# Attention and a mixture-of-experts layer on one core: query scores lead by ten pairs, two DMA loads change places on SyncE's queue, and the edges of the attention part are rewritten

## The reference

```
q, k, v = x @ w.T + b                    # 16 heads of 8 features
attn    = softmax(q . k / sqrt(8))       # 256 x 256 for each head and batch
y       = (attn @ v) @ w_o.T + b_o       # f of the first block

scores  = sigmoid(x @ gate_w.T)          # 32 experts in 8 groups
choice  = scores + e_bias                # best 4 groups, then best 6 experts
c       = scores of the 6 / their sum * 2.5
f of the second block = sum_e c[e] * relu(x @ up[e])^2 @ down[e]  +  the same with one shared expert of 256
```

## Time and profile before

| | us |
|---|---|
| median of three runs (range) | 515.81 (515.64 to 517.17) |
| the profiled execution | 516.76 |
| its span, first to last instruction | 514.9 |
| TensorE busy | 467.5 (91%) |
| VectorE busy | 399.8 (78%) |
| ScalarE busy | 362.2 (70%) |
| GpSimd busy | 227.9 (44%) |
| first key scores of batch 0, of batch 1, of batch 13 | 42.50, 57.68, 223.70 |

### The profile page before, as it was taken

One profiled execution on the slowest core, in us unless ns is written; L12 is line 12 of the kernel. 1 busy time (PEld: TensorE's weight loads), 2 busy tenths in 40 slices (PEclk: granted clock), 3 DMA queues, 4 the chain that ended last, 5 costly groups with the idle time before them and its releaser, 6 DMA issues.

```text
span 514.9 us, 10734 instructions
## 1 busy us (share of the span) xinstructions
PE 467.5 (91%) x3352; PEld 269.1 (52%) x3352; DVE 399.8 (78%) x1031; ACT 362.2 (70%) x723; POOL 227.9 (44%) x546
## 2 busy tenths in 40 slices
PE   2458999999999999998899899999999999999994
PEld 1213444444444444454346566666666676766662
DVE  3678788899999989989826769597886869597453
ACT  3415788877888978887847476868868687866551
POOL 6054233325434635230103644839385674716251
PEclk9555899999999999999979899999999999999998
DMA  6544244454344444330024244435354445536421
GB/s 201 163 136 131 87 124 125 141 149 134 124 129 134 144 141 128 116 97 2 5 87 164 87 164 164 168 114 199 94 171 158 162 164 152 202 99 202 130 109 41
DMA packets 48280, 67.47 MB, mean 131 GB/s; under 512 B 3808, under 2 KB 34784, under 8 KB 48224
## 3 DMA queue, kind: packets, MB, share of 16 engines
q1 hardware_dynamic: 48224, 66.78, 41.3%
HBM read 51.17 MB, written 15.20 MB: 129 GB/s over the span
## 4 chain that ended last, share of the span: by engine, by line
PE 71%; DVE 15%; issue 8%; ACT 4%; POOL 1%; DMA 0%; POOLq 0%; DVEq 0%; ACTq 0%
PE pO L1304 9%; PE pY L1387 8%; PE pS L1246 8%; PE pS L1387 8%; DVE mneg L920 7%; PE pS L1371 6%; PE pS L1373 6%; PE pS L1372 6%; PE pS L1252 2%; PE pX L1231 2%; PE pY L1321 2%; PE pX L1234 2%; PE pY L1333 1%; DVE q_rest L900 1%; PE pX L1226 1%
## 5 line engine op out<-in xcount | busy, mean ns | idle before, releaser
L920 DVE TENSOR_REDUCE mneg<-pS 128x2 f32<-128x512 f32 x256 | 162.7, 685 | 17.2 <-PE pS L1246 16.5
L702 ACT ACTIVATE probs<-pS 128x512 f32<-128x512 f32 x256 | 142.5, 595 | 26.5 <-PE pS L1252 24.8
L1246 PE MATMUL pS<-qk 48*128 48x256 bf16 x512 | 88.9, 289 | 20.4 <-DVE mneg L920 10.9
L1252 PE MATMUL pS<-qk 51*128 51x256 bf16 x512 | 89.9, 281 | 1.7 <-ACT probs L702 1.5
L788 ACT ACTIVATE h_ring<-r 128x512 f32<-128x512 f32 x104 | 65.0, 625 | 35.1 <-DVE r L1090 26.1
L1371 PE MATMUL pS<-qk,up_hi 128*128 128x512 f32 x144 | 88.8, 617 | 0.0
L1304 PE MATMUL pO<-probs,vv 128*32 128x256 f32 x1024 | 74.0, 396 | 0.0
L1246 PEld LDWEIGHTS pS<-qk 48*128 48x128 bf16 x512 | 33.5, 96 | 73.8 <-DVE mneg L920 48.7
L1090 DVE SCALAR_TENSOR_TENSOR r<-pS,probs 128x512 f32<-128x512 f32 x64 | 43.4, 687 | 23.0 <-PE pS L1373 22.5
L1090 DVE SCALAR_TENSOR_TENSOR r<-pS,c_ring 128x512 f32<-128x512 f32 x64 | 44.0, 688 | 17.0 <-PE pS L1373 14.6
L1373 PE MATMUL pS<-qk,up_lo 128*128 128x512 f32 x144 | 57.1, 397 | 0.0
(11 more groups left out here) (190 smaller groups left out, 823.3 us busy)
## 6 DMA issues: line engine op xcount, KB each, us to landing
c_ring<-c_scratch SPq DMA_DIRECT2D x32, 512.0 KB, 4.0
probs<-c_scratch SPq DMA_DIRECT2D x32, 512.0 KB, 3.8
qk<-qk_scratch SPq DMA_DIRECT2D x64, 192.0 KB
qk_scratch<-q_parts SPq DMA_DIRECT2D x16, 192.0 KB, 2.3
qk_scratch<-k_parts SPq DMA_DIRECT2D x16, 192.0 KB, 2.1
qk_scratch<-q_parts SPq DMA_DIRECT2D x16, 128.0 KB, 2.2
qk_scratch<-k_parts SPq DMA_DIRECT2D x16, 128.0 KB, 2.0
out_x<-probs SPq DMA_DIRECT2D x7, 256.0 KB, 4.8
```

The costliest lines, as they stand in the source:

```text
L702: nc.scalar.activation(probs[j][:, hh], pS2[n % S2_RING][:, :, :], ACT.Exp, scale=SCALE).then_inc(exp_done, 1)
L920: nc.vector.tensor_reduce(mneg[u % 2][:, :, hh, k], pS1[n % S1_RING][:, :].rearrange("p (a s) -> p a s", a=TH), AX.X, ALU.max, negate=True ...
L1246: return mm(pS1[n % S1_RING][:, T * th:T * (th + 1)], qp[slot][rows, k, P * th:P * (th + 1)], kp[slot][rows, k, :], start=True, stop=True)
L1252: return mm(pS2[n % S2_RING][:, sh], kp[slot][rows, k, P * sh:P * (sh + 1)], qp[slot][rows, k, :], start=True, stop=True)
```

## The change

- **Lead.** `LEAD` counts pairs, and is 10 instead of 12. Query scores of head pairs signal head by head in the prologue.
- **SyncE's queue.** `load_unit(2b+6)` now stands ahead of `load_max(2b+2)`; in the prologue `write_parts(1)` stands ahead of `load_unit(1)`, `load_unit(3)` behind `load_max(0)`, and `load_max(1)` goes to batch 0.
- **Places in a batch.** `project_y` goes to `j` 0 of the batch two after its own, instead of `j` 7 of the batch one after it, the transposes of the maxima of unit `2b+2` to `j` 4 and of unit `2b+3` to `j` 7, into the bank `pY` instead of `pX`. GpSimd's norms and chains are moved by half a batch.
- **Prologue.** 26 matmuls on zeros before and between the first projections (`warm_up`), separate signals for q and k, and k in a bank of its own.
- **Last batches.** A third bank for the last key scores, routing of tile 0 from the start of batch 13, and the first two up-blocks of tile 0 within the end of the attention.
- **Unmasked parts.** The high part of x and of the up-weights is ScalarE's rounded copy without the bit mask before it; the low part of the weights is subtracted by GpSimd (`low_up`), two batches later, and VectorE has no `cut_up`.
- **c.** The router's weights are laid out so that one transpose does for a tile, instead of four.

The core of the diff:

```diff
-LEAD = 3
+LEAD = 10
+S2_LATE, N_LATE = 3, H * (NB - 1)
@@ SyncE, prologue
             load_unit(0)
+            write_parts(1)
             load_unit(1)
-            write_parts(1)
             load_unit(2)
-            load_unit(3)
             write_parts(2)
             load_max(0)
+            load_unit(3)
             load_unit(4)
-            load_max(1)
@@ SyncE, batches
             for b in range(NB):
+                if b == 0:
+                    load_max(1)
                 if 2 * b + 5 < NU:
                     load_unit(2 * b + 5)
                 if b + 3 < NB:
                     write_parts(b + 3)
+                if 2 * b + 6 < NU:
+                    load_unit(2 * b + 6)
                 if 2 * b + 2 < NU:
                     load_max(2 * b + 2)
-                if 2 * b + 6 < NU:
-                    load_unit(2 * b + 6)
                 if 2 * b + 3 < NU:
                     load_max(2 * b + 3)
@@ GpSimd, units
-                if u % 2 == 0 and u >= 2:
-                    if u // 2 + 3 < NB:
-                        norm_x(u // 2 + 3)
-                    if u // 2 + 2 < NB:
-                        part2(u // 2 + 2)
-                        part3(nc.gpsimd, pool.wait_ge, u // 2 + 2)
+                if u % 2 == 1:
+                    if u // 2 + 4 < NB:
+                        norm_x(u // 2 + 4)
+                    if u // 2 + 3 < NB:
+                        part2(u // 2 + 3)
+                        part3(nc.gpsimd, pool.wait_ge, u // 2 + 3)
+                    if CUT_BATCH + 2 <= u // 2 < CUT_BATCH + 2 + NCUT:
+                        low_up(u // 2 - CUT_BATCH - 2)
@@ ScalarE, batches
-                    if s == 5 and not last:
+                    if s == 1 and b == 0:
+                        keep_mT(1)
+                    if s == 9 and not last:
                         keep_mT(2 * b + 2)
@@ VectorE, batches
-                    u = 2 * b + LEAD + s // 8
+                    u, k = divmod(NBLK * b + s // 2 + LEAD, UB)
                     if u < NU:
-                        row_max(u, s % 8 // 2, s % 2)
+                        row_max(u, k, s % 2)
-                    if s == 11 and CUT_BATCH <= b < CUT_BATCH + NCUT:
-                        cut_up(b - CUT_BATCH)
@@ TensorE
             def scores_by_query(u, k):
                 for hh in range(2):
                     query_scores_free(u, k, hh)
-                for th in range(TH):
-                    for hh in range(2):
+                    for th in range(TH):
                         ins = query_scores(u, k, hh, th)
-                        if th == TH - 1:
-                            ins.then_inc(s1_done, 1)
+                    ins.then_inc(s1_done, 1)
             def transpose_c(i):
                 pe.wait_ge(c_done, i + 1)
-                for c in range(C4):
-                    ins = tr(pX[0:E, P * c:P * (c + 1)], root_c[:, c], idf[:, :])
-                ins.then_inc(cT_done, 1)
+                tr(pX[:, 0:P], root_c[:, :, :].rearrange("p e c -> p (e c)"), idf[:, :]).then_inc(cT_done, 1)
+            pe.wait_ge(warm_set, 1)
+            warm_up(14)
...
+                if b < 2:
+                    warm_up(6)
...
+                    if j == 0 and b >= 2:
+                        pe.wait_ge(mT_kept, 2 * b + 2)
+                        project_y(b - 2)
                     if j in (0, 1) and b >= 1:
                         for sh in range(TH):
                             outputs(b - 1, 2 + j, sh)
...
                     if j == 7:
-                        if b >= 1:
-                            project_y(b - 1)
+                        if last:
+                            project_y(b - 1)
+                        else:
+                            pe.wait_ge(*((onT_kept, b) if b >= 1 else (v_kept, 2)))
+                            transpose_max(2 * b + 3)
                         if proj:
-                            pe.wait_ge(mT_kept, 2 * b + 4)
+                            pe.wait_ge(mT_kept, 2 * b + 3)
                             project_q(b + AHEAD)
                             project_k(b + AHEAD)
             for sh in range(TH):
                 outputs(NB - 1, 2, sh)
+            up_block(0, 1)
+            for sh in range(TH):
+                outputs(NB - 1, 3, sh)
```

More of the change, by code:

```diff
@@ L235, in block_kernel @@
         tiny_set = sem("tiny_set")
+        warm_set = sem("warm_set")
+        q_part1, q_rest_done, q_part2 = (sem(n) for n in ("q_part1", "q_rest_done", "q_part2"))
         preset = sem("preset")
@@ L585, in split_down, with low_up @@
                                         ALU.subtract).then_inc(dlo_done, 1)
+            def low_up(c):
+                pool.wait_ge(whi_done, c + 1)
+                blocks = slice(CUT * c, min(CUT * (c + 1), FBLK))
+                nc.gpsimd.tensor_tensor(up_lo[:, blocks].rearrange("p a b -> p (a b)"), up_in[c],
+                                        up_hi[:, blocks].rearrange("p a b -> p (a b)").bitcast(F32),
+                                        ALU.subtract).then_inc(wlo_done, 1)
             def low(i, s):
@@ L834, in _ @@
                         keep_cT(0)
-                    if s == 8 and last:
+                    if s == 4 and b == NB - 2:
                         high_x(0)
@@ L840, in _ @@
                         keep_xT(0)
-                    if s == 7 and b == NB - 3:
+                    if s == 0 and b == NB - 3:
                         exp_logits(0)
@@ L899, in rest @@
                 for i, (left, parts) in enumerate(((q_rest, q_parts[b % 2]), (k_rest, k_parts[b % 2]))):
-                    ins = nc.vector.scalar_tensor_tensor(out=left[:, :], in0=pX[:, T * i:T * (i + 1)],
+                    if i == 1 and b < AHEAD:
+                        dve.wait_ge(part1_done, b + 1)
+                    ins = nc.vector.scalar_tensor_tensor(out=left[:, :], in0=qk_bank(b, i),
                                                          scalar=bqk_sb[:, i:i + 1], in1=parts[:, 0],
                                                          op0=ALU.add, op1=ALU.subtract)
+                    if i == 0 and b < AHEAD:
+                        ins.then_inc(q_rest_done, 1)
                 ins.then_inc(rest_done, 1)
@@ L1124, in _ @@
             dve.wait_ge(xq_loaded[2], 16)
-            for t in range(FIRST, FIRST + NT // 3):
-                nc.vector.bn_stats(stats[:, t, :], xbig[:, t])
+            for t in range(FIRST, SECOND):
+                ins = nc.vector.bn_stats(stats[:, t, :], xbig[:, t])
+            ins.then_inc(ln1_stats, 1)
             rest(1)
             part3(nc.vector, dve.wait_ge, 1)
-            for t in range(FIRST + NT // 3, NT):
+            for t in range(SECOND, NT):
                 ins = nc.vector.bn_stats(stats[:, t, :], xbig[:, t])
@@ L1132, in _ @@
             rest(2)
-            for u in range(LEAD):
-                for k in range(UB):
-                    for hh in range(2):
-                        row_max(u, k, hh)
-                    if u == 1 and k == 0:
-                        rest(AHEAD - 1)
+            for p in range(LEAD):
+                u, k = divmod(p, UB)
+                for hh in range(2):
+                    row_max(u, k, hh)
+                if p == UB + 2:
+                    rest(AHEAD - 1)
             rt = Link(dve, rt_link, 0)
@@ L1180, in _ @@
                         route(rt, i + 1, ROUTE_AT[i >= 1].index(k))
-                    if i + 1 < NTILE and k == 14:
-                        cut_x(i + 1)
+                    if i + 1 < NTILE and k == 12:
+                        low_x(i + 1)
                     if i == 0 and k == 0:
@@ L1414, in transpose_f, with warm_up @@
                 ins.then_inc(f_done, 1)
+            def warm_up(n):
+                for _ in range(n):
+                    mm(pS2[0][:, :, :].rearrange("p a b -> p (a b)"), xT[:, 0:P // 2].bitcast(BF16),
+                       xT[:, 0:T].bitcast(BF16), start=True, stop=True)
+            pe.wait_ge(warm_set, 1)
+            warm_up(14)
             pe.wait_ge(wqk_loaded, 16 * N_WQK)
@@ L1492, in _ @@
                         outputs(b, 1, 0)
+                        if last:
+                            pe.wait_ge(max_done, H * NB)
+                            up_block(0, 0)
                     if j == 6:
@@ L1519, in _ @@
                     n = FBLK * i + k
-                    up_block(i, k)
+                    if n >= 2:
+                        up_block(i, k)
                     downs(n)
-                    if i == 0 and k == 0:
-                        for sh in range(TH):
-                            outputs(NB - 1, 3, sh)
                     if i == 0:
```

241 lines of the change are left out of this document (113 added, 128 removed).

## The result

The changed kernel takes 563.48 us (median of four runs, 560.17 to 566.26) against 515.72 for the kernel before (515.42 to 517.17): ratio 1.092, 95% interval 1.085 to 1.098. Forecast were 553.5, with 531 to 570 as range: it is slower, by the stretch that was named, and most of the 10 us more lies behind batch 13. The profiled execution has a span of 561.9.

A forecast was written before the change was run, and what follows sets the result against it. SyncE's once-a-batch queue chain was taken to set a 17.9 us period (16.5 plus 1.4 clock). Batch 1 at 52.0 plus 214.2 gives 266.2; adding 291.2, less 3 and 1.8, gives 552.6 of span, 553.5 median; range 531 to 570.

The forecast's parts named there:

- The deciding term: SyncE's queue: maxima behind a unit load that waits for the parts' landing make a once-a-batch chain, 16.5 us before clock surcharge.
- The upper bound of the landing: Maxima queued behind the unit's bytes land 6.0 to 6.7 us after the unit's issue, at 16.0 to 16.6 in the batch.
- The period of 17.9: Each of twelve periods from batch 1 to 13: a chain of 16.5 us plus 1.4 for the lowered clock.
- rival 1: Chain decides, but TensorE's clock stays up or recovers before the next batch: period 16.5, total 537; chance 0.22.
- the forecast's: At the chain's head, TensorE's clock stays low after the wait, adding 1.4 us a batch (0 to 2.1); chance 0.60.
- The bound of 18.6: Upper bound in us of the forecast period for the chain through SyncE, with 14.1 as the lower.
- The prologue: Two pairs fewer save 3.2 us and separate loads and signals 4.8, so batch 0 begins at 34.5 (33 to 38).
- Batch 0 to 1: The same queue chain at a low clock makes this stretch 17.5 us (15.5 to 18.5) instead of 15.2.
- the term for batches 13 to the end: The chain ends; earlier routing and up-blocks change the time by -3 us, the second block by -1.8.
- The second block's own part: One transpose of `c` instead of four saves 0.26 us for each of seven tiles: -1.8 us.
- "VectorE without `cut_up`": With `project_y`'s new place, would save up to 13.83 against about 13.2 per period; nothing under the longer chain.
- Rival 3: Faster: the small maxima load passes the unit's bytes, period 14.1 and 508, or 13.2 and 497; chance 0.12.

The follow-up runs named there:

- a_max_first: The changed kernel with the next batch's first maxima loaded ahead of the unit on SyncE's queue again: 519.03 us, ratio 1.007 to the kernel before.
- the corrected kernel: The changed kernel with maxima loaded ahead of the unit (519.03 us); moving GpSimd's low part of the weights behind the first split gave 515.24 us.
- a corrected kernel: The changed kernel with maxima ahead of the unit, tile 0's routing later and GpSimd's low part behind the second split: 507.65 us, ratio 0.986 to before.

## Why the prediction was right

**The deciding term** held by its steps. The upper bound of the landing (6.0 to 6.7 behind the unit's issue, from the prologue's 6.0 and the traffic) measured 6.57 in batch 3 and 6.29 in the mean, and the price of the order alone was 36 us in the kernel before and 44.5 in the changed one. The period of 17.9 was 17.90 on average; so close a hit is luck, since the terms behind it were off in both directions. In the mean of the twelve batches VectorE's rest was ready 5.08 after the head (4.04, and 1.4 for the clock, had been taken), the unit went out 6.54 later (5.91), and the next head came 6.29 after that (6.55). So the clock cost 1.0 a batch. The average also hides two states. In windows of one batch each, batches 8 to 10 have a clock of 0.98 to 1.00 and take 16.62, 15.94 and 18.49; the other nine have 0.82 to 0.90 and take 16.48 to 20.23. In batch 7, too, the first four us have 1.00, so at the chain's head rival 1's mechanism held in four batches and the forecast's in eight. The wait of about 2 to 4 us was there at eight of the twelve heads; at those of batches 7 to 10 it was under 1.4, and TensorE waited 0.8 to 1.5 for GpSimd's split of the maxima within the batches before them. The bound of 18.6 was passed in batches 2, 3 and 6: in batch 2 the writes landed 3.1 behind the end of their issue, where 1.3 had been taken, and in 3 and 6 the six took 4.5 and 4.6 to issue instead of 3.0. In batch 10 they landed 3.0 behind it (223.70 to 226.70). The maxima took 5.0 us from issue to release behind a unit in batch 3 (4.0 to 5.3 in the twelve rounds), and 2.8 to 3.3 without one ahead. With this the trace agrees with the Trainium skill ("DMA: Bandwidth & Descriptors", section "Queues, rings and completion order") that descriptors are taken in ring order. By the semaphore events a first piece of batch 4's maxima arrived at 107.41, ahead of the unit's last piece (110.80), but TensorE waits for their last one, at 111.15. The slices of the earlier trace rows are 0.225 us wide, and not half a microsecond, as the prediction reads them.

**The prologue** came as said: batch 0 at 35.07 (34.5), 7.4 earlier than before. Batch 0 to 1 took 18.88 (17.5).

**Where it was off** is the term for batches 13 to the end: forecast -3 and -1.8, that is 286.4 of 291.2 left; measured 561.9 - 268.80 = 293.1. These 6.7, with 1.4 from batch 0, 0.6 from batch 0's beginning and 0.6 in the periods, are the 9.3 of span that the forecast missed. The second block's own part was right, and a bit better (0.32 a tile instead of 0.26). The transition was mis-sized: batches 13 and 14 take 18.03 and 14.74, where before they took 13.58 and 13.42, and from batch 15 on 3.9 are saved. Half clock behind the last wait costs some 2 (first score to value projection 5.85 in batch 13, 3.9 before), and routing at heads 2 and 4 holds the row maxima up, which was worth 3.1 in `a_max_first`, where I had put earlier routing down as a gain only. The wait of 1.15 that it was to remove is 0.34 here, and 1.17 in `a_max_first`. "VectorE without `cut_up`" had been counted at nothing under the longer chain; that was right, but its other half, the low part that GpSimd takes over, I had not followed through GpSimd's queue: 3.8 in the corrected kernel. And the saving in each period that was to come without the chain (13.2) did not: a plain batch is at 13.69, 0.3 above before, because of GpSimd's order.

Rival 3 decides from a period of 14.8 downwards; the shortest of the twelve was 15.94.

What stays open: why the same writes land 1.2 to 3.1 us after the end of their issue, why their issue took 1.5 longer in batches 3 and 6, and how much of the 2.8 to 3.3 us, from issue to release without a unit ahead, is the load itself.

## What to carry to other kernels

When an instruction is moved in an in-order queue, ask what the instruction that it passes waits for, and whether that wait depends on work of the same round; if so, the queue has become a cycle, whose length is a lower bound of the period. A share of idle time on an engine off the path says nothing about this: SyncE's and GpSimd's orders, at 42% busy for GpSimd, were worth 44 and 31 us. And a saving that only a corrected kernel shows (here 1.4%, won up to batch 1 and behind batch 13, none of it in the twelve periods between) is found by undoing the costly places one by one, here three of them, not by throwing the change away.

## What the runs showed that was not expected

A wait at the head of a round costs more than its own length: 4.4 us of wait were followed by four us of full work at 1.2 GHz, in the stretch that the next wait hangs on, and the rest was ready 2.0 later for it: one wait helps to make the next. Filling the wait with idle work bought 7.6 us where the waits were long, and the fill in batches 6 to 10 lost 8.2 (564.08 against 555.93).
